# Diagonal score tiles of 128 and 256 columns: several heads in one bank, mask by TensorE, one maximum for all

## The reference, cut to what matters

```python
h = _L0_tok_ref(x, L0_tok_W)                       # (8, 1024, 128)
# attention of layernorm(h)
Q = split_heads(x @ Wq + bq)                       # (8, 8 heads, 1024, 16)
K = split_heads(x @ Wk + bk)
V = split_heads(x @ Wv + bv)
scores = jnp.einsum('bhqd,bhkd->bhqk', Q, K)
causal = jnp.tril(jnp.ones((n, n), dtype=jnp.float32))
mask = (1.0 - causal) * -100000.0
attn = jax.nn.softmax((scores + mask) / math.sqrt(d), axis=-1)
out = jnp.einsum('bhqk,bhkd->bhqd', attn, V)
h = h + out @ Wo + bo
# then layernorm, shared SwiGLU, top-2 of 8 experts in the chosen group, and h = h + both
```

## Time and profile before

| what | value |
|---|---|
| median of 3 runs | 942.92 us (940.74 to 944.81) |
| the profiled execution | 941.0 us, its span 939.0 us |
| instructions | 17,696 |
| granted TensorE clock, mean | 0.99 |

### The profile page before, as it was taken

How to read it: one execution, slowest core, us unless ns; L and a number is a source line. 1 busy time by engine, 2 the same in 40 slices (tenths; PEclk the granted TensorE clock), 3 DMA queues, 4 the chain that set the end, 5 groups by cost and what they waited for, 6 DMA issues and landing times.

```text
span 939.0 us, 17696 instructions
## 1 busy us (share of the span) xinstructions
PE 900.1 (96%) x5646; PEld 535.8 (57%) x5646; DVE 784.4 (84%) x2529; ACT 597.2 (64%) x1365; POOL 376.2 (40%) x526
## 2 busy tenths in 40 slices
PE   6788999899999999999999999999999999999996
PEld 5633355356665756456555656466565755555675
DVE  6889997998789799989889898998889998894543
ACT  3235676567766675776767675776767675776734
POOL 3713413323545335433364235534354224422434
PEclk9879999999999999999999999999999999999999
DMA  5311101200101011110021101110011011000000
GB/s 188 65 36 49 37 26 35 77 8 4 49 30 64 2 36 37 64 38 26 10 67 50 35 10 38 52 37 28 27 61 35 13 44 37 19 19 13 1 12 23
DMA packets 45980, 35.19 MB, mean 37 GB/s; under 512 B 10816, under 2 KB 44608, under 8 KB 45760
## 3 DMA queue, kind: packets, MB, share of 16 engines
q1 hardware_dynamic: 43680, 31.97, 10.7%
q10 hardware_dynamic: 2208, 2.10, 0.8%
HBM read 4.28 MB, written 4.19 MB: 9 GB/s over the span
## 4 chain that ended last, share of the span: by engine, by line
PE 84%; DVE 10%; ACT 2%; issue 2%; ACTq 1%; DMA 0%; SPq 0%; POOL 0%; POOLq 0%; DVEq 0%
PE bank_w L594 14%; PE bank_p L576 13%; PE bank_s L546 13%; PE bank_f L682 6%; PE bank_f L684 6%; PE bank_f L683 6%; PE bank_f L480 3%; PE bank_f L482 3%; PE bank_f L481 3%; PE bank_m L648 3%; DVE bank_s L784 3%; DVE mx_far L780 3%; PE bank_m L622 2%; PE bank_m L612 1%; PE bank_m L632 1%
## 5 line engine op out<-in xcount | busy, mean ns | idle before, releaser
L1051 ACT ACTIVATE pt<-bank_p 128x512 f32<-128x512 f32 (+3 forms) x768 | 350.0, 492 | 184.4 <-PE bank_p L576 160.2
L784 DVE CUSTOM_DVE_ANT_0 bank_s<-bank_s,causal 128x384 f32<-128x384 f32 (+3 forms) x512 | 244.7, 506 | 39.1 <-PE bank_s L546 35.9
L546 PE MATMUL bank_s<-k_stack,q_stack 96*128 96x512 bf16 (+3 forms) x768 | 236.0, 334 | 15.7 <-DVE mx L784 7.8
L576 PE MATMUL bank_p<-q_stack,k_stack 99*128 99x512 bf16 (+3 forms) x768 | 228.7, 332 | 4.1 <-ACT pt L1051 3.0
L780 DVE TENSOR_REDUCE mx_far<-bank_s 128x1 f32<-128x512 f32 x256 | 166.2, 683 | 21.5 <-PE bank_s L546 19.5
L1213 POOL TENSOR_SCALAR_AFFINE_SELECT pt<-pt 128x512 f32<-128x512 f32 x128 | 81.9, 641 | 221.5 <-ACT pt L1051 221.3
L594 PE MATMUL bank_w<-pt,v 128*32 128x512 f32 (+3 forms) x1536 | 154.9, 497 | 0.3 <-ACT ot L1042 0.2
L546 PEld LDWEIGHTS bank_s<-k_stack,q_stack 96*128 96x128 bf16 x768 | 72.3, 99 | 134.2 <-DVE mx L784 57.0
L576 PEld LDWEIGHTS bank_p<-q_stack,k_stack 99*128 99x128 bf16 x768 | 71.6, 99 | 113.2 <-ACT pt L1051 68.5
L682 PE MATMUL bank_f<-wex_h,hid_h 128*128 128x512 f32 x256 | 116.5, 455 | 0.8 <-DVE gate L936 0.7
L684 PE MATMUL bank_f<-wex_h,hid_l 128*128 128x512 f32 x256 | 101.3, 396 | 0.0
(11 more groups left out here) (139 smaller groups left out, 1417.8 us busy)
## 6 DMA issues: line engine op xcount, KB each, us to landing
q_stack<-qk_h SPq DMA_DIRECT2D x96, 64.0 KB, 2.6
k_stack<-qk_h SPq DMA_DIRECT2D x84, 64.0 KB, 2.6
q_stack<-qk_m SPq DMA_DIRECT2D x64, 64.0 KB, 2.6
out<-h SPq DMA_DIRECT2D x16, 256.0 KB, 2.5
k_stack<-qk_m SPq DMA_DIRECT2D x56, 64.0 KB, 2.6
q_stack<-qk_l SPq DMA_DIRECT2D x32, 64.0 KB, 2.6
k_stack<-qk_l SPq DMA_DIRECT2D x28, 64.0 KB, 2.4
x_sb<-x_t SPq DMA_DIRECT2D x16, 64.0 KB, 2.2
```

What stands on the lines that cost most here:

```text
L546: nc.tensor.matmul(s_bank[s % 2][:, 0:cols], q_stack[0:STACK, half, hd, t % HT * P:(t % HT + 1) * P], k_stack[0:STACK, hd, key_place(i, ha ...
L576: nc.tensor.matmul(p_bank[p % 2][:, q0:HALF], k_stack[:, hd, key_place(i, kt // HT), kt % HT * P:(kt % HT + 1) * P], q_stack[:, half, hd, ...
L784: nc.vector.tensor_tensor_reduce(src, src, causal[:, HALF - cols:HALF], 1.0, -3.0e38, ALU.add, ALU.max, mx[:, u, col:col + 1]).then_inc(s_ ...
L1051: nc.scalar.activation(pt[:, k % PT_SLOTS, j, q0:HALF], p_bank[p % 2][:, q0:HALF], ACT.Exp, scale=0.25).then_inc(exp_done, 1)
```

## The change

Tiles on the diagonal with 128 columns take all four heads of the group in one step, those with 256 columns two heads. The heads lie side by side in the same score bank, so that such a bank always holds 512 columns. Behind each head's matmul TensorE adds the triangle to the last 128 columns of that head, by a second matmul of `ident_b` with `later_b` (the identity and the triangle in bf16, 128 columns, accumulated). VectorE then takes one plain `tensor_reduce` for the four or the two heads. Tiles of 384 and 512 columns stay as they were. A unit's 16 diagonal steps become 11 (1 + 2 + 4 + 4); the program's 768 score steps become 608. There are 256 more matmuls (8 a unit). GpSimd makes the two bf16 tiles in `constants`, and TensorE waits for them in the first batch.

```diff
 SCORES = [(u, HT * half + t, j, diag) for u, (g, half) in enumerate(UNITS)
-          for diag in ((0, 1) if half else (1,)) for t in range(HT) for j in range(G4)]
+          for diag in ((0, 1) if half else (1,)) for t in range(HT) for j in range(0, G4, HT // (t + 1) if diag else 1)]
...
+        ident_b, later_b = sb("ident_b", [P, P], BF16), sb("later_b", [P, P], BF16)
...
                 cols = (t % HT + 1) * P if diag else HALF
-                nc.tensor.matmul(s_bank[s % 2][:, 0:cols], q_stack[0:STACK, half, hd, t % HT * P:(t % HT + 1) * P],
-                                 k_stack[0:STACK, hd, key_place(i, half if diag else 0), 0:cols],
-                                 start=True, stop=True).then_inc(s_ready, 1)
+                many = HT // (t % HT + 1) if diag else 1
+                if i == 0 and many > 1:
+                    pe.wait_ge(masks_made, 2)
+                for m in range(many):
+                    mm = nc.tensor.matmul(s_bank[s % 2][:, m * cols:(m + 1) * cols],
+                                          q_stack[0:STACK, half, hd + m, t % HT * P:(t % HT + 1) * P],
+                                          k_stack[0:STACK, hd + m, key_place(i, half if diag else 0), 0:cols],
+                                          start=True, stop=many == 1)
+                    if many > 1:
+                        mm = nc.tensor.matmul(s_bank[s % 2][:, (m + 1) * cols - P:(m + 1) * cols], ident_b[:], later_b[:],
+                                              start=False, stop=True)
+                mm.then_inc(s_ready, 1)
...
                 cols = (t % HT + 1) * P
+                many = HT // (t % HT + 1)
+                if many > 1:
+                    nc.vector.tensor_reduce(mx[:, u, 0:ROWS].rearrange("p (j t) -> p j t", t=HT)[:, j:j + many, t % HT],
+                                            s_bank[s % 2][:, 0:many * cols].rearrange("p (j c) -> p j c", c=cols),
+                                            AX.X, ALU.max).then_inc(s_taken, 1)
+                    return
...
                 pool.wait_ge(const_made, CONSTS)
+                nc.gpsimd.tensor_copy(ident_b[:], ident[:]).then_inc(masks_made, 1)
+                nc.gpsimd.tensor_copy(later_b[:], causal[:, HALF - P:HALF]).then_inc(masks_made, 1)
+                pool.wait_ge(masks_made, 2)
```

More of the change, by code:

```diff
@@ L149 @@
[L149 to L153, removed]
@@ new lines @@
+        "psssswsesppsppsptssspsppwppsspsppspspspbspppbsswwbwsbpsswppapspwppsbswssppbsfsppfpfpswppftpfpwpfspsfafss"
+        "ppfssfbsswsbsppfbpfbpfppssbppsfpsstppwwpphwspspbswspbspappfpfppfbwwppefpspfspspfpspwppwppsfspspfsppappsf"
+        "sfppsapspfsphspsftspfwwwsppfbfssppbfpspbpsfbpspsfapswpswsppwwppsasppswpsptppssppespwwpspbsspwspsaspsffsp"
+        "bffspasppfpswpffppswppfbfpbfbppfssbfpsbpsfsppshpwpspsfbspwwspptfsppffppsbppsfspfsppsfspaspwwspspfwppsspf"
+        "ptwwpssfpafppfspaspspfspspasfsppsbfsshpsfsstfspsfsesppsfwwwspspapspwsppwpssppapspspwspspwspspwppsbspsppw"
@@ new lines @@
+        "pspspbpwpspsptpswpspbsppswsbppssppeppsspwppapspwpsspwpbwsspbppfssppfpapfwwpbpfbfsfbpsfbppfspfpbpsfpshspf"
+        "ssppfbsftppssfsbfspsaffpspsaspwwwwpsspfppftsppfpspafpfspapsspfpsspfpsspwwwwspspfssppfpsspbfppsshspspwssf"
+        "spstfppssfsffpssppewwwpspbpsppspbsppwppsbpspwpspsbsppwwspepspsppasppwpssppwspptwssppbswssasspffapsspffsb"
+        "sppffppsafppswwppfbfbpsfpspbfssbfpbpspsfpphpsfbspswwpptwpspbsppffppsapspfppsswsppwwsppsfppsfspfpsptfpspa"
+        "pswwwppfssppfpsspfpsasppsfsspfpsspasppfbsfsshssftsfsspfssefsppwwppwwspassppwspspappsswpspbpspswpspbpspps"
@@ new lines @@
+        "ptpwspspbwpspsbpspspapspwsppwpspapspwpbspswspsbspfppwpbfpfbppfspbfpspfbfsppfbpfspshppsfbssfssbfptfespsww"
+        "wppwpspsfpbfppsfpsasfppsfsppapsspfpswwwptfpspawsppfspfpspsappsfspwspwwssppfpstfsspfsppfppsshpsspfsppsfps"
+        "psfspspfssfspewwwwppsspppsbppwspbspwppsappsswpsppbswsbpspptpssppwppsapwppsppspwppsbspswspsapssffppssbpfs"
+        "peffssppfappfwwwpsfspspbfsbppsfbfbpspsfhsppfspsptfbpsfpspfsapwwwppsbsswsppsasppfspptfwppfbppsspappswppfs"
+        "swwpsbpfpspassppfspfsppsfpspswspspwwsppstfppssffspsfpssfppsfpssphppwwsppswppsfsfsppbpswsppsbppsspbpspsbp"
@@ new lines @@
+        "sbssassstssssssasffsasffssbfafbsbfbsbfsbfbssasbbsfsbhssssftsbbasbssfssfsabssfssftssfsabfssfssfsfssssasfa"
+        "sssfsshssstssfsseasfasssasssassbsssbssstssssbsbssasbassssssbbbbfsfbbfsfbffsffsbbssbhsfsssssbtfbbbessabss"
+        "fasfssassfssafstsfafssfssasfssfssfsstssfssshsfssssfsssfsseassabssbsssasssssbsbstssbasssssssssafssfbfsfef"
+        "fbbsasfsbsbsfbafbssassfsshstsbfsbfsbasssssssaftfsbsbsbbsbsfafsssfsssfsssssasfssfssfsstsfsssshsfsssfssbss"
+        "bsssssbbstssssbssssssssbbfbfsbffbsfsfsffssssfsssfsstbbbbbhfbfbbfbfffffffbbbfbbfbhffbffbffbfbfffbffhff"
@@ L199 @@
+        "fcapcacapcapcppppcppppabpabffapapbcbpcpfafcpccapcappcapppcpbppppbaaffabcapbcpppafcfacapcpcapcpppcpppapbp"
+        "pabffbpacpacbcppfafapccpaccppappcppppbppabaffaaccppbpbpacfapcfppppcpccpcpppbppbffppppbcbacppcfppfcbccbff"
         "cccccc"
@@ L201 @@
     "sp": (
[L202 to L203 removed]
+        "eeideddtdetdtdddtedtdddtcetdddtddctdddtcetdddtddctdetdtcddeeddtddcdtddtctddtddeddctddtedctddeetdtdctddtc"
+        "dddddtddtcdtctdtccc"
     ),
```

70 lines of the change are left out of this document (24 added, 46 removed).

## The result

The changed kernel takes 949.04 us (median of 9 runs, 944.75 to 951.39) against 942.69 us of the kernel before on the same chip: a ratio of 1.0056, 95% interval 1.0042 to 1.0070. It is slower by 0.6% by this ratio; the medians alone stand 6.4 us (0.7%) apart, where the forecast was 1.0 us. The profiled executions stand 8.3 us apart (spans 947.3 and 939.0).

A forecast was written before the change was run, and what follows sets the result against it. TensorE's own work was taken to bound the kernel from 200 us on. 11.5 - 3.0 - 3.0 - 4.5 = +1.0 us on 942.9 gave 943.9 us; own range 938 to 949, with the rivals 930 to 954 us.

The forecast's parts named there:

- the steady part: From the ninth unit to the last, about 200 us on: forecast 8.5 us slower (11.5 - 3.0).
- the start: Stretches ahead of the ninth unit, 24 to 200 us: a gain of 7.5 us was forecast (4.5 + 3.0).
- What bounds the kernel: From 200 us on TensorE's own work sets the time; VectorE's share comes mainly from the first 200 us.
- Masks, +11.5 us: From 200 us on: 192 mask matmuls on TensorE at 0.06 us each, covered by nothing, +11.5 us.
- the second rival: Each accumulating mask matmul on TensorE costs 0.11 us, sum +10.8 us, 953.7 us; chance 0.15.
- Relief from 200 us on, -3.0 us: 200 to 870 us: of 17.3 us freed on VectorE only about TensorE's visible waits come back, -3.0 us.
- The start, -4.5 us: 24 to 55 us: VectorE saves 1.4 us and its 2.8 us wait for TensorE ends, -4.5 us.
- From 55 to 200 us, -3.0 us: Some 6 units scored: VectorE freed by 4.3 us, TensorE's idle time takes most of 48 masks, -3.0 us.
- The moved letters, 0 with 3 either way: Order strings of the engines: the same steps, about as often alternating, so 0, with 3 us either way.
- The POOL copies at nothing: Two GpSimd copies in `constants`: needed by TensorE's first score only at 24 us, so cost 0.
- VectorE as the pace throughout, faster: Rival: VectorE sets the pace over the whole span, so its freed time comes back, 921 to 935 us; chance 0.30.
- The third rival: VectorE's grouped maximum is no cheaper than the pairs (0.84 us each), +10 us, 953 us; chance 0.08.

## Why the prediction held in its wide range and was wrong in its parts

The median of 949.04 us lies in the range of 930 to 954 us, but that range was stretched to take in the rivals; the forecast's own ended at 949. Slower by over 0.5% had a chance of 0.25, the least of the three outcomes, and it came, if barely (0.42 to 0.70%). That the time came out within some 5 us of the forecast is in part luck: the steady part was forecast 1.6 us too long, the start 9.0 us too short, of which 1.35 lie ahead of the change.

**What bounds the kernel.** "From 200 us on the time is TensorE's own work" holds for relief as far as the traces show: two kernels that freed VectorE and gave TensorE no more work (9.8 and 15.3 us of busy time freed) have steady parts of -1.0 and 0.0 us. But it does not mean that VectorE had room; that conclusion, drawn from 87% busy and 3.0 us of visible waits, was wrong. Each us put on VectorE in the kernel before came out as 0.5 to 0.7 us in the steady part. As I read it, the two engines are locked to each other by fixed strings and a few shared banks: slowing either costs, and speeding up one mostly leaves the other. No run loosened the strings or added a bank, so this reading is not shown.

**Masks, +11.5 us: right in kind, too large by over a third.** From the ninth unit on 184 masks cost 6.9 us; 192 by that rate are 7.2. The start-to-start price of 0.06 us is right, and the second rival, 0.11 us each, is refuted by the rows at 406.80 to 406.97. The estimate by the Trainium skill (TensorE: Matmul & The Clock Gate, the back-to-back issue gap), 81 ns and 15.6 us, lies further off than the row; the row was the better guide. What both lack is that a part of the masks' time was taken from TensorE's idle time.

**Relief from 200 us on, -3.0 us: too large, it was about 0.** The visible waits for a score bank went from 1.5 to 0.7 us; those for a prob bank stayed (1.5 and 1.6). The two errors cancel in part, which is luck: 8.5 us were forecast for the steady part, 6.9 came.

**The start, -4.5 us: this is the step that failed.** I argued that VectorE "waits for TensorE 2.8 us, because one head at a time comes over", and that four heads at once would end that wait. VectorE's waits from 20 to 55 us in the changed kernel (against the earlier trace rows):

```profile
DVE mx L792 <- PE bank_s L553: 3.4, 3, 2.3
DVE bank_s L797 <- PE bank_s L548: 1.3, 2, 0.9
DVE h L727 <- PE bank_m L506: 1.1, 1, 1.1
```

They are 5.8 us now for TensorE, 4.7 of them for scores, where 2.8 were. TensorE in order of time shows the longest of them:

```profile
27.39 0.31 PE L553 MATMUL bank_s<-later_b,ident_b 128*128 128x128 bf16 x1
27.49 2.02 PE L506 MATMUL bank_m<-tokw_sb,x_sb 128*128 128x128 f32 x8
30.39 1.09 PE L514 MATMUL bank_m<-ident,z 128*128 128x128 f32 x4 [0.88 <-DVE h L727]
31.27 0.64 PE L490 MATMUL bank_f<-ident 128*128 128x128 f32 x2
31.70 0.42 PE L548 MATMUL bank_s<-k_stack,q_stack 96*128 96x256 bf16 x1
...
32.23 0.31 PE L553 MATMUL bank_s<-later_b,ident_b 128*128 128x128 bf16 x1
```

Between the second and the third joined step TensorE's string has the embedding and a transposition, and the third maximum on VectorE starts only at 32.58, 2.3 us late. With single heads eight steps lay there to be spread around such pieces; a joined step leaves VectorE one long instruction and then nothing. I had seen in the order that "the embedding has moved behind the second step" and cost it at nothing. The clock makes it longer. From 28 to 32 us it was granted at 0.50, the lower of its two levels, where it was 0.92 before; the same eight matmuls of the embedding took 2.02 us here, and in the kernel before:

```profile
24.29 1.17 PE L508 MATMUL bank_m<-tokw_sb,x_sb 128*128 128x128 f32 x8
```

The first prob step, forecast some 4 us earlier, is 0.2 us earlier, and 1.5 us earlier counted from the first score. Its exponential in the kernel before, and then in the changed one:

```profile
55.65 1.89 ACT L1051 ACTIVATE pt<-bank_p 128x512 f32<-128x512 f32 x3 [9.47 <-PE bank_p L576]
```

```profile
55.49 0.60 ACT L1064 ACTIVATE pt<-bank_p 128x512 f32<-128x512 f32 x1 [9.05 <-PE bank_p L583]
```

**From 55 to 200 us, -3.0 us: failed too.** The waits for the score banks that were to go (3.9 us) are 4.1 us in the changed kernel:

```profile
PE bank_s L548 <- DVE mx_far L787: 2.5, 9, 0.5
...
PE bank_s L548 <- DVE mx L797: 1.6, 6, 0.3
```

By the ninth unit 1.5 us are lost instead of 7.5 gained, 1.35 of them ahead of the first score. Part of this is the clock: 31 × 0.22 + 145 × 0.06 = 15.5 us of it are missing from 24 to 200 us, against 31 × 0.11 + 145 × 0.04 = 9.2 before. I had given that 0.02 and no price. With the clock up again (extra matmuls for three units) and a first score at 23.94 us the ninth unit is 2.1 us ahead of before; without the masks too it is 4.3 us ahead. So of the missing gain about 2 us are the clock and 2 the masks of the start. The remaining 3 us I put down to the order of joined steps, which no run shows: none moved the embedding back alone.

**The moved letters, 0 with 3 either way: too small.** They are worth 5.7 us; without them the change would have cost 12 us.

**The POOL copies at nothing** held: the second of them ends at 16.8 us, 8.7 us before the first score.

```profile
16.48 0.29 POOL L1194 CAST later_b<-causal 128x128 bf16<-128x128 f32 x1
```

**The rivals.** VectorE as the pace throughout, faster (921 to 935 us), did not come: even without paying for the masks the kernel's median is 940.2, and its fastest run 936.2. So the rule of the Trainium skill that I set beside it (Perfetto Trace Analysis, on the most-contended engine) would have promised too much here: weight loads were 57% busy and VectorE 84%, and relieving VectorE of 15.3 us brought 2.8, some 5 at like clock, while the masks that paid for it cost 8.9. Yet the rival was right in one thing that I denied, that VectorE's time counts when it grows. The third rival, the grouped maximum as dear as the pairs, is refuted by 684 ns.

## What to carry to other kernels

Freeing an engine and loading it are two different measurements: here either engine cost 0.6 to 0.9 us per us added, and VectorE gave back 0.1 to 0.3 us per us of busy time taken from it. So a change that moves work from one to the other can pay on the new engine without being paid on the old one; the new order won 5.7 us of that back. Joining small steps into large ones saves instructions, but takes away the pieces with which a consumer was kept supplied at the start; look at what stands between two joined steps before counting the gain. And where a kernel's runs spread with the granted clock, compare runs at like clock before saying that nothing was gained.

## What the runs showed of the hardware that was not expected

At a granted clock of 1.00, the successor of a bf16 matmul of 128 columns that adds into the columns that the matmul just before it wrote starts 0.06 us after it, as that of one that writes other columns does (406.80 to 406.97). A maximum over 512 columns of a score bank takes 683 or 684 ns whether it gives one, two or four results, and 680 ns from `causal` in place of a bank. And a mean granted clock lower by 0.008 in a run went with some 5 us of time in the changed kernel, though its profiled execution, at 0.981, shows 1.00 from 200 to 870 us: what it lacks lies ahead of 200 us but for the last microseconds, so it must be there that a run with a higher clock differs. No trace of such a run was kept.
